# The sum of the experts' two outputs moves from VectorE to GpSimd

## The reference: what is computed

```python
# layer 0 (a shared expert is added too)      # layer 1
scores = softmax(x @ gate_w.T); top 2 of 8     scores = x @ Wg.T; top 2 of 8
out = sum over the 2 chosen e: w[e] * expert_e(h)
x = x + gb * out                               # gb: one row of 128 per batch
```

## Time and profile before

| | |
|---|---|
| three runs | 1306.59, 1314.46, 1316.88 us |
| median | 1314.46 us |
| the profiled execution | 1314.97 us, of which the span of its trace 1313.7 us |
| busy over the span | PE 960.4, DVE 859.1, ACT 687.3, POOL 375.1 us |
| sum of layer 0 (first add to last statistics) | 830.39 to 858.7 us |
| sum of layer 1 (first add to last x) | 1289.81 to 1307.25 us |

### The profile page before, as it was taken

The page is one execution under the profiler, slowest core; times in us unless marked ns, Lnnn a source line. Parts: engine busy times, 40 slices in busy tenths (PEclk is TensorE's granted clock), DMA queues, the critical chain, the costliest instruction groups (busy, mean ns, idle before and its releaser), DMA issues. The chain is left out here.

```text
span 1313.7 us, 26786 instructions
## 1 busy us (share of the span) xinstructions
PE 960.4 (73%) x9029; PEld 615.8 (47%) x9029; DVE 859.1 (65%) x2070; ACT 687.3 (52%) x1428; POOL 375.1 (29%) x448
## 2 busy tenths in 40 slices
PE   5563789999999999866887999029667460799990
PEld 2231233333333333244554898017464350699990
DVE  5695788888888888257553666694394871244444
ACT  4441377777777777743544777075112230466660
POOL 0004012211221122113554677100000377344440
PEclk9785699999999999996898999558778555799995
DMA  6352011100010000002211333400652432222216
GB/s 182 83 184 95 2 50 32 41 30 26 31 42 29 26 26 2 2 1 71 63 48 57 92 100 89 136 1 1 175 153 65 100 100 69 54 64 65 65 57 198
DMA packets 113389, 88.90 MB, mean 68 GB/s; under 512 B 16413, under 2 KB 103640, under 8 KB 113000
## 3 DMA queue, kind: packets, MB, share of 16 engines
q1 hardware_dynamic: 100328, 67.11, 18.3%
q0 software_dynamic: 8704, 17.97, 4.0%
q10 hardware_dynamic: 4224, 2.10, 0.5%
HBM read 56.05 MB, written 30.82 MB: 66 GB/s over the span
## 5 line engine op out<-in xcount | busy, mean ns | idle before, releaser
L821 DVE TENSOR_REDUCE part<-sps 128x2 f32<-128x1024 f32 (+2 forms) x320 | 341.7, 1114 | 64.7 <-PE sps L702 42.8
L796 ACT ACTIVATE prob<-tpa 128x1024 f32<-128x1024 f32 (+1 forms) x208 | 193.1, 928 | 75.2 <-PE tpa L738 72.8
L1502 POOL DMA_INDIRECT yk<-yo,place x144 | 145.9, 1013 | 127.9 <-ACT yo L1531 104.7
L641 POOL TENSOR_SCALAR_AFFINE_SELECT prob<-prob 128x512 f32<-128x512 f32 x128 | 79.7, 634 | 354.2 <-ACT prob L796 354.2
L796 ACT ACTIVATE prob<-tpb 128x512 f32<-128x512 f32 (+1 forms) x224 | 128.2, 572 | 62.6 <-PE tpb L738 62.5
L758 PE MATMUL ops<-prob,vs 128*32 128x512 f32 (+3 forms) x1536 | 158.5, 500 | 1.5 <-POOL prob L641 1.5
L1144 POOL DMA_INDIRECT xg<-h,slot x128 | 125.9, 983 | 98.0 <-DVE slot L1216 60.8
L695 PE MATMUL sps<-qk 48*128 48x512 bf16 (+3 forms) x768 | 135.4, 343 | 22.8 <-DVE part L821 22.0
L1557 DVE COPY place<-xt 128x1 uint32<-128x1 uint32 x144 | 22.0, 153 | 157.7 <-ACT esg L1525 122.8
L1614 PE MATMUL banks<-xT,y 128*128 128x128 f32 x864 | 109.7, 277 | 0.6 <-ACT y L1516 0.6
L1614 PEld LDWEIGHTS banks<-xT,y 128*128 128x128 f32 x864 | 103.9, 194 | 0.9 <-issue 0.9
(11 more groups left out here) (319 smaller groups left out, 1770.7 us busy)
## 6 DMA issues: line engine op xcount, KB each, us to landing
xt<-xg SPq DMA_DIRECT2D x144, 65.0 KB, 1.9
h<-yk SPq DMA_DIRECT2D x32, 256.0 KB, 4.6
qk<-term SPq DMA_DIRECT2D x24, 256.0 KB, 3.4
qk<-qk SPq DMA_DIRECT2D x64, 96.0 KB
arena<-kpad SPq DMA_DIRECT2D x6, 1024.0 KB, 11.3
qk<-qk SPq DMA_DIRECT2D x64, 64.0 KB
rows_w<-in_w SPq DMA_DIRECT2D x16, 176.0 KB
yk<-yo,place POOLq DMA_INDIRECT x144, 2.4
```

Source lines behind the costliest of these rows:

```text
L641: nc.gpsimd.affine_select(out=blk, in_=blk, pattern=[[0, HQ], [1, P]], compare_op=ALU.is_ge, fill=0.0, base=0, channel_multiplier=-1).then ...
L796: nc.scalar.activation(prob[:, at:at + len(units), 0:n], slot_of(t, m)[:, :, 0:n], ACT.Exp, scale=float(HD) ** -0.5).then_inc(exp_done, 1)
L821: freed(nc.vector.tensor_reduce(to, src, AX.X, ALU.max, negate=True))
L1502: nc.gpsimd.indirect_dma_start(out=d.yk, out_offset=bass.IndirectOffsetOnAxis(ap=place[:, u:u + 1], axis=0), in_=yo[u][:], in_offset=None) ...
```

## The change

The add of a step's two outputs leaves DVE and is done by POOL, in a new part `gpsimd_part` of `combine_parts` at the end of POOL's stream of each layer. POOL waits for the loads (`got[u]`) and counts up a new semaphore `summed`; DVE waits for `summed` in place of `got[u]` and then applies the gate and adds to x as before. The loads and stores and what they wait for are unchanged.

```diff
@@ -1655,6 +1655,7 @@
            for k in range(2)]
     got = [sem(f"got{u}") for u in range(4)]
     c_step, x_done, stored, var_done, root_done = sem("c_step"), sem("x_done"), sem("stored"), sem("c_var"), sem("c_root")
+    summed = sem("summed")
 
     def sync_part(sp):
         for u in range(UN):
@@ -1667,14 +1668,20 @@
                 at = k * TOK + s * ST
                 sp.dma_start(gat[k][u], d.yk[at:at + ST, :].rearrange("(j p) c -> p j c", p=P)).then_inc(got[u], 16)
 
+    def gpsimd_part(pool):
+
+        for s in range(2 * NB):
+            u = s % 4
+            pool.wait_ge(got[u], 16 * 2 * (s // 4 + 1))
+            nc.gpsimd.tensor_tensor(gat[0][u], gat[0][u], gat[1][u], ALU.add).then_inc(summed, 1)
+
     def vector_part(dve):
         v = nc.vector
         link = Chain(dve, c_step)
         for s in range(2 * NB):
             u, b = s % 4, s // 2
-            dve.wait_ge(got[u], 16 * 2 * (s // 4 + 1))
-            a0, a1 = gat[0][u], gat[1][u]
-            link(v.tensor_tensor(a0, a0, a1, ALU.add))
+            dve.wait_ge(summed, s + 1)
+            a0 = gat[0][u]
             link(v.tensor_tensor(a0, a0, w.gate[:, 2 * layer + 1, b:b + 1, :].to_broadcast([P, 4, C]), ALU.mult))
             v.tensor_tensor(w.x[:, 4 * s:4 * s + 4, :], w.x[:, 4 * s:4 * s + 4, :], a0, ALU.add).then_inc(x_done, 1)
             if layer == 0 and s % 2 == 1:
@@ -1698,7 +1705,7 @@
             act.wait_ge(stored, 16 * 2 * NB)
 
     made = Work()
-    made.sync, made.vector, made.scalar = sync_part, vector_part, scalar_part
+    made.sync, made.vector, made.scalar, made.gpsimd = sync_part, vector_part, scalar_part, gpsimd_part
     return made
 
 
@@ -1724,6 +1731,7 @@
                     experts.clear(pool)
                 routed.gpsimd(pool)
                 experts.gpsimd(pool)
+                combined.gpsimd(pool)
 
             @block.vector
             def _(dve):
```

## The result

The changed kernel takes 1321.88 us in the median against 1314.46 of before (13 runs each): a ratio of 1.0054, 95% interval 1.0041 to 1.0068, which is 5.4 to 8.9 us slower, 7.1 at the ratio itself. That is within 1%, and slower by its interval. One run of before, at 1379.88 us, was slow and is left out of the ratio. The profiled execution took 1322.48 us, its span 1321.2.

The account below looks back on a forecast made before the run. DVE was taken to bound the two sums, some 46 us of a 1313.7 us span. Layer 1 +3.5 and layer 0 +0.5 make +4.0 on the median 1314.46: 1318.5 us, range 1308 to 1325.

Parts of the forecast that it names:

- exclusion of the two engines: In both layers' sums, POOL's add and a DVE instruction nearly never run together; +4.0 us in all, chance 0.72.
- the two rows: POOL's same operation at 128x128 (448 ns) and 128x1024 (2338 ns); the line between them gave 1.26 us at 512 elements.
- a scatter that was stretched to 1.45 us: POOL scatter, 0.96 us undisturbed, 1.45 us beside DVE's L1165 and L1166; taken as the nearest evidence for hindrance.
- Layer 1, +3.5: Sum of layer 1: seven steps of 2.64 us, 18.5 against 14.5, +4.0; or +2.7 with fixed add time hidden; +3.5 taken.
- Layer 0, +0.5: Sum of layer 0: 2 of 7 adds free beside statistics, 26.0 us against 24.9, +1.1; +0.5 taken.
- the fixed 0.18 us of an add: Length-independent part of each POOL add; hidden beside DVE, it takes 1.3 us off layer 1 and 0.9 off layer 0.
- rival 3: At the edges, a layer's first add starts late after 72 scatters; worth at most 1 us, no chance given.
- Rival 1: No hindrance, adds hide: layer 0 -4.0 us, layer 1 +0.4 because loads bind, total 1310.9 us; chance 0.23.
- Rival 2: Adds slow to 1.9 us beside DVE, all on the path: layer 0 +8.1, layer 1 +8.5, total 1331 us; chance 0.05.

Follow-up runs that it names:

- r6: Changed kernel, but POOL clears the second tile with a same-size memset instead of adding, leaving the second output out of the result; ratio to before 0.9978.
- r7: Changed kernel, but POOL copies the first tile into the second instead of adding; one run without interval, layer 0 28.8 us, layer 1 21.2 us.
- r3: Kernel before plus one POOL memset of 128x8 elements in layer 1 after the last x, no add moved; ratio to before 1.0032.
- r5: Changed kernel, with the adds of steps 6 and 7 of layer 1 back on DVE; ratio to before 1.0035.
- r8: Kernel before, but POOL adds steps 2, 4 and 6 of layer 0 only, each started by the x ahead of a statistics; ratio to before 1.0007.

## Why the prediction was right, and where it was off

The forecast was slower by 4.0 us, within 1%, for exclusion of the two engines; measured were 7.1 us, in the range and on the forecast side, and the forecast mechanism makes 3.1 of the 4.8 us that the rows show. That the number came so near is in part luck: layer 1 was put 1.4 us too high, layer 0 0.5 too low, and the 1.7 us of the end were missing; and 2 us of the 7.1 have no known cause. Point by point:

1. **POOL's add costs 1.26 us**: right to the hundredth (1.26 where it is alone), from the line through the two rows.
2. **The engines exclude each other**: right. It was taken from a scatter that was stretched to 1.45 us; that row leaned the right way, but it was weak evidence: another scatter of the same line, from 1057.35, has the whole of an L1166 (1057.47, 0.69 us) beside it and takes 0.96, and how much a scatter reads is shown nowhere. The proof is in the adds and x of the changed kernel, and r6 and r7 show that POOL's reading is what excludes.
3. **Layer 1, +3.5**: mechanism right, size too large. Computed were +4.0 for seven steps, taken +3.5; from step 1's add on the profiles show +2.1. The steps were put at 2.46 to 2.64 us and are 2.27 to 2.39: the taking of turns overlaps at its edges. The add of 1304.99 ends at 1306.64, so its undisturbed 1.26 us would have begun at 1305.38, 0.14 us ahead of the end of the gate (1304.84 + 0.68); x is then done at 1307.19, 0.55 us after the add and not 0.69; and the next gate starts 0.07 us ahead of the end of x. That is 0.14 + 0.14 + 0.07 = 0.35 us a step, and 2.64 less 2.28 is 0.36. The last step has no add behind its gate at all.
4. **Layer 0, +0.5**: computed was +1.1, and +0.5 taken on the guess that the fixed 0.18 us of an add can hide. From step 1's add on it is +0.8 in the profiled pair and +1.0 over all profiles, so the computed value was right and the deduction was not. Two adds of seven were said to be free. Two lie beside a statistics in the profile after, but those of steps 3 and 4, not 4 and 6, and the second of them holds L99: POOL takes the data as it comes, and those of steps 5, 6 and 7 met a gate or x.
5. **The end of the program**: missing. The prediction says of the wait on POOL that nothing is queued behind it but the next add, and of rival 3 that things at the edges are worth at most 1 us. What is queued behind the last add is POOL's drain, in both kernels and over by 1290.7 in before. Moving work to POOL moved it to the end, +1.7 us. r3 produced it with one memset of 0.1 us, and r5 took it away again. This is the step that failed; with it the forecast would have been +5.7.
6. **Rival 1**, no hindrance: wrong in its condition, right in its consequence for layer 1. r6, without exclusion, has layer 1 at 21.3 us with the DMA engines full, and layer 0 4.6 us shorter (computed: 4.0; from step 1's add 25.6 - 21.1 = 4.5).
7. **Rival 2**, adds of 1.9 us all on the path: adds reach 1.81, but that length is the other side's turn and not added to it.

## What to carry to other kernels

Before an elementwise instruction is moved to POOL to relieve DVE, look at what DVE does at that moment: beside instructions that read two tiles from SBUF the two engines take turns, so the total is what counts, and an add of 1.26 us on POOL is no relief for one of 0.68 on DVE. It could hide beside L97, which reads one tile (r8), where it was started there on purpose; but one instruction with one input, L104, was held in r7, so look at the rows. And look at what follows the last instruction of the engine that gets the work: here POOL needs 6 us from its last instruction to the exit of the block, which costs nothing early in the block and 1.7 us at its end.

## What the runs showed of the hardware

- POOL's drain at a block's exit is over 6.03 to 6.05 us after the end of its last instruction, whatever that was: a scatter (before), an add (changed), a memset of 8 elements a partition (r3).
- A DVE instruction with two SBUF inputs (0.69 us) that starts while POOL reads is done 0.54 to 0.55 us after POOL's end. It is held by an add and by a copy, not by a memset of 0.52 us.
- Instructions of DVE as small as 0.17 us are held too: L99, two inputs of 8 elements, took 1.04 and 1.07 us beside an add, and L104, one input of 8 elements, took 0.59 us beside a copy (r7, once).
- L97, one input, is not held and does not hold: 1.64 us beside an add of 1.26 (r8).
